# A mixer's parts over thirteen groups at a time, and another order inside a group, in an attention phase on one core

## What is computed

```python
# graph attention (8 heads of 32)
score = einsum('ehd,ehd->eh', q[edge_dst], k[edge_src])
score = clip(score / sqrt(32), -10, 10)
ex    = exp(score - smax[edge_dst])
den   = segment_sum(ex, edge_dst)
wv    = segment_sum(ex / den[edge_dst] * v[edge_src], edge_dst)
# ball mixer, from the same normalized rows, one sequence position
h   = relu(batchnorm(conv(logmap0(proj(x)))))
cat = concat([t, pointwise(depthwise(t))])        # t from h
vk  = einsum('ngdl,ngel->ngde', v, relu(k))
out = einsum('ngde,ngdl->ngdl', vk, relu(q)) / (sum(v) + 1e-15)
fx  = proj(expmap0(logmap0(proj(expmap0(out))) @ w_res + b_res))
```

## Time and profile before

| | us |
|---|---|
| median of 3 runs | 3400.9 (3397.17 to 3411.24) |
| the profiled execution | 3413.5 |
| its span in the trace | 3411.8 |
| mean granted TensorE clock | 0.859 |
| busy: PE / PE weight loads | 2540.0 (74%) / 2051.8 (60%) |
| busy: DVE / ACT / POOL | 2133.1 (63%) / 1269.2 (37%) / 1238.6 (36%) |

### The profile page before, as it was taken

How to read it: one execution, slowest core, us unless ns; L and a number is a source line. 1 busy time by engine, 2 the same in 40 slices (tenths; PEclk the granted TensorE clock), 3 DMA queues, 4 the chain that set the end, 5 groups by cost and what they waited for, 6 DMA issues and landing times. The chain is left out here.

```text
span 3411.8 us, 62980 instructions
## 1 busy us (share of the span) xinstructions
PE 2540.0 (74%) x17412; PEld 2051.8 (60%) x17412; DVE 2133.1 (63%) x4254; ACT 1269.2 (37%) x2593; POOL 1238.6 (36%) x971
## 2 busy tenths in 40 slices
PE   6546555777579999766767686767655976999997
PEld 5424344666457777543656564656544865899986
DVE  7655455644468888754686867777775566444455
ACT  1432211311245455423535353444433343444441
POOL 0058786688400000002646464655623001211125
PEclk9968855888779999777979898888977986999998
DMA  5238574233100000044647465555634004466633
GB/s 142 84 85 222 143 206 122 67 82 83 42 19 19 10 18 18 25 148 126 159 112 170 121 163 131 152 149 141 160 94 117 0 0 162 147 237 226 236 121 87
DMA packets 251663, 387.61 MB, mean 114 GB/s; under 512 B 117456, under 2 KB 175661, under 8 KB 246878
## 3 DMA queue, kind: packets, MB, share of 16 engines
q0 software_dynamic: 151392, 170.67, 20.5%
q1 hardware_dynamic: 87224, 202.62, 18.9%
q10 hardware_dynamic: 12864, 12.06, 1.2%
HBM read 323.76 MB, written 60.56 MB: 113 GB/s over the span
## 5 line engine op out<-in xcount | busy, mean ns | idle before, releaser
L921 POOL DMA_INDIRECT ms_got<-gather,edge_src x400 | 531.1, 1328 | 164.7 <-issue 120.2
L2120 POOL DMA_INDIRECT xz_rows<-gather_kv,edge_src x205 | 257.5, 1256 | 220.5 <-PE ab_total L2292 165.2
L2120 POOL DMA_INDIRECT ab_gkv<-gather_kv,edge_src x200 | 266.5, 1333 | 187.6 <-PE ab_total L2292 132.9
L969 PE MATMUL ms_total<-ms_got,ms_hot 125*125 125x256 f16 x1040 | 177.3, 335 | 177.4 <-DVE ms_hot L942 126.8
L969 PEld LDWEIGHTS ms_total<-ms_got,ms_hot 125*125 x1040 | 150.3, 171 | 212.2 <-issue 211.8
L1635 ACT ACTIVATE ex_h<-ex_up,ex_now 128x313 f32<-128x313 f32 (+1 forms) x320 | 196.1, 613 | 196.7 <-PE ex_up L700 189.3
L3027 DVE CAST moe_hidden<-moe_h 128x256 f16<-128x256 f32 (+1 forms) x336 | 101.5, 302 | 203.6 <-ACT moe_h L2964 201.0
L2266 PE MATMUL ab_picked<-y_rows,ab_zeros 125*125 125x512 f16 (+1 forms) x246 | 73.8, 417 | 204.6 <-DVE ab_qk L2365 184.4
L1851 POOL MEMSET br_one<- 125x1 f16 x1 | 0.1, 106 | 604.4 <-POOLq L125 604.4
L2964 ACT ACTIVATE moe_h<-moe_up,wring 128x256 f32<-128x256 f32 (+1 forms) x336 | 163.1, 487 | 128.6 <-PE moe_up L700 85.7
L2275 PE MATMUL ab_picked<-y_rows,xz_rows 125*125 x1060 | 178.0, 329 | 35.6 <-issue 18.0
(11 more groups left out here) (527 smaller groups left out, 6090.3 us busy)
## 6 DMA issues: line engine op xcount, KB each, us to landing
wring<-wsplit SPq DMA_DIRECT2D x33, 2052.0 KB
ab_dsts<-in_dst SPq DMA_DIRECT2D x83, 305.2 KB
wsplit<-mix_split SPq DMA_DIRECT2D x32, 512.0 KB
mix_raw<-in_L_ffn_W1p SPq DMA_DIRECT2D x16, 512.0 KB
mix_raw<-in_L_ffn_W2p SPq DMA_DIRECT2D x16, 512.0 KB
results<-moe_made SPq DMA_DIRECT2D x32, 256.0 KB, 7.6
ms_got<-gather,edge_src POOLq DMA_INDIRECT x400
gather_kv<-qkv_out SPq DMA_DIRECT2D x5, 1120.0 KB
```

The source lines that it names most:

```text
L921: pool.indirect_dma_start(out=self.got[:, s, j, :], out_offset=None, in_=self.m.gather0, in_offset=bass.IndirectOffsetOnAxis(ap=self.m.edg ...
L969: ins = pe.matmul(self.total[:, visit % 2, 0:C], self.hot[:, visit % RING, j, :], self.got[:, s, j, p * C:(p + 1) * C], start=(j + p == 0) ...
L2120: pool.indirect_dma_start(out=gkv[s][:, j, 0:2 * C], out_offset=None, in_=m.gather_kv, in_offset=bass.IndirectOffsetOnAxis(ap=m.edge_src[: ...
```

## The change

Nothing is computed in another way. Two things are laid out anew.

First, the stages. PERIOD is 13 and a chunk now has 27 stages, so that two chunks (three at one group of each period) are in work at once: `chunks_at(n)` lists them, older first. JOIN, WEIGH, OUT and LAST take every second group. The seven DVE operations of a weighing are divided over three groups: four at the stage, the reciprocal one group later, the last two products two groups later; `ksum` has two buffers for that. At multiples of 13 a stage 0, a reciprocal (stage 13) and a tail (stage 26) come together.

Second, the order within a group. DVE weighs and makes the one-hots of n before it multiplies for n + 1; PE makes the totals of n before the picks of n + 2. ACT keeps its order.

```diff
-    PERIOD = G // CHUNKS
-    CONV, JOIN, WEIGH, OUT, LAST, TAIL = 0, 3, 8, 9, 10, 15
+    PERIOD = 13
+    CONV = range(0, 3)
+    JOIN, WEIGH, OUT, LAST = (range(at, at + 2 * J, 2) for at in (3, 12, 15, 17))
+    ROOTS, TAIL = 25, 26
+
+    def chunks_at(n):
+        return [(c, n - c * PERIOD) for c in range(CHUNKS) if 0 <= n - c * PERIOD <= TAIL]
...
-        ksum = ph.sb("ksum", [R, GN])
+        ksum = ph.sb("ksum", [R, 2, GN])
...
-                    if g % PERIOD == CONV + 8 and g // PERIOD < CHUNKS - 1:
-                        sp.wait_ge(s_up, g // PERIOD * UNITS + len(PARTS) * OB)
-                        rows(g // PERIOD + 1)
-                    if g % PERIOD == 6 and 0 < g // PERIOD < CHUNKS:
-                        mixed(g // PERIOD - 1)
+                    for c in range(CHUNKS - 1):
+                        if g == c * PERIOD + 8:
+                            sp.wait_ge(s_up, c * UNITS + len(PARTS) * OB)
+                            rows(c + 1)
+                        if g == c * PERIOD + TAIL + 4:
+                            mixed(c)
...
                 for n in range(G):
-                    part(n // PERIOD, n % PERIOD)
+                    for c, s in chunks_at(n):
+                        part(c, s)
                     bounds = group_bounds(act, m, n + 3)
                     weights(n + 1, (n + 1) % GATHERED)
                     one_hots(n + 3, (n + 3) // 2, (n + 3) % 2, bounds)
...
                 for n in range(G):
-                    c, s = divmod(n, PERIOD)
                     ahead = group_bounds(pe, m, n + 2)
                     bounds = group_bounds(pe, m, n)
-                    part(c, s, False)
+                    for c, s in chunks_at(n):
+                        part(c, s, False)
+                    sums(n, n % GATHERED, bounds)
                     pick_q(n + 2, ahead)
-                    part(c, s, True)
-                    sums(n, n % GATHERED, bounds)
+                    for c, s in chunks_at(n):
+                        part(c, s, True)
...
                 def late(c, s):
-                    if s == WEIGH:
+                    for j, at in enumerate(WEIGH):
+                        q, w = cat[:, j, 0, :, :], cat[:, j, 2, :, :]
+                        if s == at + 1:
+                            b.link(dve.reciprocal(w, w))
+                        if s == at + 2:
+                            b.link(dve.tensor_tensor(q, q, w, ALU.mult))
+                            b.link(dve.tensor_tensor(q, q, repeat_last(ksum[:, j % 2, :], HD), ALU.mult))
+                            b.done(s_o)
+                    if s == WEIGH[0]:
...
-                        b.link(dve.reciprocal(w, w))
-                        b.link(dve.tensor_tensor(q, q, w, ALU.mult))
-                        b.link(dve.tensor_tensor(q, q, repeat_last(ksum[:, :], HD), ALU.mult))
-                        b.done(s_o)
...
                 for n in range(G):
-                    c, s = divmod(n, PERIOD)
-                    early(c, s)
-                    multiply(n + 1)
+                    for c, s in chunks_at(n):
+                        early(c, s)
                     weigh(n)
                     bounds = group_bounds(dve, m, n)
-                    visits(n, s, bounds)
+                    visits(n, n, bounds)
+                    multiply(n + 1)
                     scores(n + 1)
-                    late(c, s)
+                    for c, s in chunks_at(n):
+                        late(c, s)
```

More of the change, by code:

```diff
@@ L11 @@
+import itertools
 from contextlib import ExitStack, contextmanager
@@ L2182, in weights, with squared @@
                         .then_inc(s_exp, 1)
-                def squared(source, into, before):
-                    act.wait_ge(s_square, before + AHEAD)
+                squares = itertools.count(AHEAD)
+                def squared(source, into):
+                    done = next(squares)
+                    act.wait_ge(s_square, done)
                     act.activation(junk[:, 0:source.shape[-1]], source, ACT.Square, accum_out=into)\
                         .then_inc(s_square, 1)
-                SQUARES = 4 * J + J + J
+                    return done + 1
                 def convolved(c, u):
@@ L2201, in joined @@
                     bank = unit[0:R, u % 2, 0:HALF]
-                    squared(bank, s2[:, k, j:j + 1], c * SQUARES + (j * 4 + k))
+                    squared(bank, s2[:, k, j:j + 1])
                     parts = bank.rearrange("p (g q d) -> p q g d", q=3, d=HD)
@@ L2207, in part @@
                 def part(c, s):
-                    if CONV <= s < CONV + 3:
-                        for u in range(4 * (s - CONV), 4 * (s - CONV) + 4):
+                    if s in CONV:
+                        for u in range(4 * s, 4 * s + 4):
                             convolved(c, u)
-                    if JOIN <= s < JOIN + J:
+                    if s in JOIN:
                         for k in range(4):
-                            joined(c, s - JOIN, k)
-                    if s == WEIGH:
+                            joined(c, JOIN.index(s), k)
+                    if s == WEIGH[0]:
                         act.wait_ge(s_sum, c + 1)
                         act.activation(nr[:, 0:2, :], s2[:, 1:4:2, :], ACT.Sqrt).then_inc(s_norm, 1)
-                    if LAST <= s < LAST + J:
-                        j = s - LAST
+                    if s in LAST:
+                        j = LAST.index(s)
                         t = c * J + j
@@ L2224, in part @@
                         act.activation(fx[:, j, :], o_bank[0:R, 0:C], ACT.Copy).then_inc(s_raw, 1)
-                    if OUT <= s < OUT + J:
-                        j = s - OUT
+                    if s in OUT:
+                        j = OUT.index(s)
                         t = c * J + j
@@ L2230, in part @@
                                        ACT.Copy).then_inc(s_oc, 1)
[L2231 to L2234, removed]
+                        turned[c] = squared(cat[:, j, 0, :, :].rearrange("p g d -> p (g d)"), s2[:, 4, j:j + 1])
+                    if s == ROOTS:
+                        act.wait_ge(s_square, turned[c])
                         act.activation(nr[:, 2, :], s2[:, 4, :], ACT.Sqrt).then_inc(s_norm2, 1)
@@ L2238, in part @@
                             act.wait_ge(s_fx, c * J + (j + 1))
-                            squared(fx[:, j, :], s2[:, 5, j:j + 1], c * SQUARES + (5 * J + j))
-                        act.wait_ge(s_square, c * SQUARES + (6 * J + AHEAD))
+                            done = squared(fx[:, j, :], s2[:, 5, j:j + 1])
+                        act.wait_ge(s_square, done)
                         a_.link(act.activation(nr[:, 3, :], s2[:, 5, :], ACT.Sqrt))
                         act.activation(nr[:, 4, :], nr[:, 3, :], ACT.Tanh).then_inc(s_tanh, 1)
+                turned = {}
                 act.wait_ge(s_node, 3)
@@ L2315, in part @@
                 def part(c, s, late):
-                    if CONV <= s < CONV + 3:
-                        if s == CONV and not late:
+                    if s in CONV:
+                        if s == 0 and not late:
                             pe.wait_ge(s_rows, (c + 1) * 16)
                             pe.sem_inc(s_pace, 1)
-                        for u in range(4 * (s - CONV) + 2 * late, 4 * (s - CONV) + 2 * late + 2):
+                        for u in range(4 * s + 2 * late, 4 * s + 2 * late + 2):
                             convolve(c, u)
-                    if JOIN <= s < JOIN + J:
+                    if s in JOIN:
                         for k in range(2 * late, 2 * late + 2):
-                            join(c, s - JOIN, k)
-                    if LAST <= s < LAST + J and not late:
-                        t = c * J + (s - LAST)
+                            join(c, JOIN.index(s), k)
+                    if s in LAST and not late:
+                        t = c * J + LAST.index(s)
                         pe.wait_ge(s_oc, t + 1)
@@ L2331, in part @@
                         ins.then_inc(s_f, 1)
-                    if OUT <= s < OUT + J and late:
-                        j = s - OUT
+                    if s in OUT and late:
+                        j = OUT.index(s)
                         t = c * J + j
@@ L2425, in late @@
                         b.link(dve.tensor_tensor(nr[:, 6, :], nr[:, 6, :], nr[:, 5, :], ALU.mult))
-                    if WEIGH <= s < WEIGH + J:
-                        j = s - WEIGH
-                        gamma = nr[:, 6, j:j + 1]
+                    if s in WEIGH:
+                        j = WEIGH.index(s)
+                        gamma, total_k = nr[:, 6, j:j + 1], ksum[:, j % 2, :]
                         q, k, w = (cat[:, j, i, :, :] for i in range(3))
-                        b.mark(dve.tensor_reduce(ksum[:, :], k, AX_X, ALU.add))
+                        b.mark(dve.tensor_reduce(total_k, k, AX_X, ALU.add))
```

(6 more changed lines are left out.)

## The result

The changed kernel takes 3540.89 us (median of 4 runs, 3535.43 to 3549.66) against 3402.16 us for the kernel before in the same comparison: a ratio of 1.041, 95% interval 1.038 to 1.044. It is slower by 139 us, where 47 were forecast and the range ended at 3515. The direction was right, the size was a third of what came.

What follows compares the result with a forecast made beforehand. The prediction took a new ring through PE, ACT and DVE to bound the attention phase. Execution 3413.5 us, plus 24 for rings and 23 for the clock, gave 3460, or 3448 us against the runs' median; range 3375 to 3515.

Steps and rivals of the forecast that it cites:

- The new ring through PE and ACT: One-hots, totals, picks, late units, exp, weighing: join and convolution groups 10.75 us, OUT 9.73, longer than DVE's 9.3 to 9.6.
- the sum said + 24: All groups and second visits of the phase, 940 us against 913.5, less 3 at the end, with PE at full clock.
- I take + 23, a little below the middle of 0 and 88, since PE will be busy between the two: Clock's cost on 350 us of PE work in the rings: 0 at join-window clock 1.00, 88 at weighing-window clock 0.80.
- this case runs from 3395 to 3515: Bounds of the first case, chance 0.52, forecast 3448 us, from the clock's ends and 0.5 us per ring either way.
- the 29 us of the rings: Uncertainty of the ring lengths: 0.5 us either way for each of 58 rings.
- Second visits: PE goes to a second visit's first total at once: 24 times 3.94 us against some 6.0, saving about 50 us.
- The exp's wait, 50 to 90 us: Sign of being right: DVE's weighing newly waits for ACT's exp, 1 to 1.5 us in join, convolution and OUT groups.
- DMA and POOL cost nothing: Gathers get a group more to land, so DVE's 72 us of waits for them should go.
- Before, the product (n+2) went ahead on DVE while the exp came; now nothing of the next group can: On DVE, the reason given for the ring: weighing (n+1) waits for the exp with no product ahead; no separate size.
- The rival that DVE's own ring decides: Weighing on DVE, groups 12 to 75: the exp is there when DVE's late part ends; 3280 us, chance 0.20.
- The rival that the clock stays at 0.80 or second visits wait as before (0.14): PE's clock stays low, or PE is in mixer units when first one-hots come: 3500 to 3530 us, chance 0.14.
- The rival of a shorter ring: Picks overlap the totals' end, ring 0.4 us shorter, clock near 1.00: 3400 us, no change, chance 0.14.

Runs made afterwards that it cites:

- ACT's order: The changed kernel with one call moved on ACT, the next group's exp ahead of the mixer's part instead of behind it: 3403.44 us, ratio 0.999 to the kernel before.
- PE's late units: The changed kernel with PE's late mixer units moved ahead of the totals, ACT untouched: 3344.62 us, ratio 0.982 to the kernel before.
- stages alone: The changed kernel with the order inside a group put back on DVE and PE, stages spread as in the change: 3342.22 us, ratio 0.980 to the kernel before.
- ten zeros: The changed kernel with ten never-read products of zeros on PE ahead of every group's totals: 3443.93 us, ratio 1.010 to the kernel before.
- two variants of it: The changed kernel with the old order on DVE and PE (3342.22 us), and, second, with PE's late mixer units ahead of the totals (3344.62 us).

## Why the prediction was right, and where it was wrong

- **The new ring through PE and ACT**: right, and shown by three openings at different places (ACT's order 137 us, PE's late units 196 us, stages alone without it). At full clock (0.99 to 1.00 over these groups) its sum holds: OUT 9.73 forecast, 9.64 measured; join with one visit and one pick visit 10.75 forecast, 10.62 to 10.67 in four groups of the changed kernel and the same with ten zeros. A tail is 13.9 in the forecast and 13.5 to 14.1 measured, at a clock of 0.78 to 0.82. The run with ten zeros stands at + 35 where the sum said + 24; whether the other 11 are the zeros in the way is not shown. So the direction was no luck.
- **"I take + 23, a little below the middle of 0 and 88, since PE will be busy between the two"**: this step failed, the clock's term of the sum. Taking PE's idle time away with ten zeros gives 97 us back, and the change's 139 less that run's 35 is 104: the term measures some 100 us. Two things were wrong in it. First, PE is not busy between the two windows (22.0 and 18.6 us of 25) but less than in either, 17.1, since it waits 312 us for one-hots, and the clock of the phase is 0.81. The prediction's own working with 0.81 gives an estimate of + 82. Second, I spread a window's mean over 350 us of PE work, but the low clock does not fall evenly: the new order makes PE idle 3.2 us on average (311.8 us, 98 times) just ahead of the totals, which stand in the ring, and there it falls (72 of 104 at 0.50 to 0.73, 32 at 1.00). The totals alone grew by 128.5 us, while the picks gained 41 (178.0 to 136.6 us). So 88 was no upper bound for the clock.
- **"this case runs from 3395 to 3515"**: the upper end is added wrong. It has the clock's 88 but not the 29 us of the rings: 3413.5 - 12.6 + 24 + 88 + 29 = 3542, which the measured 3541 just reaches. That doesn't mend the + 23.
- **Second visits, "Against some 6.0 before this saves about 50 us"**: wrong by the same cause. The forecast was a wait of about 60 us; it was 98.6 with the slow totals, and 61.6 in the run with ten zeros.
- **The exp's wait, 50 to 90 us**: 187.8. With the zeros it is 88.8, and 42 more are idle time without a releaser.
- **DMA and POOL cost nothing**: right; gathers are waited for 17 us instead of 72.
- **"Before, the product (n+2) went ahead on DVE while the exp came; now nothing of the next group can"**: the weight was wrong. With only PE turned and the product ahead on DVE the time is 3610 us. The totals' place on PE closes the ring, not the product's.
- **The rival that DVE's own ring decides**: false of this kernel, and what two variants of it reached (groups of 8.9 to 9.7 us). Its time was too low (3280; measured 3342 and 3345), with 95 us for second visits already in it. A part is that an empty group takes 6.4 us in the second of them, where it had 5.9; the rest is open. Interleaving the two regimes by the stages alone gains 2.0%.
- **The rival that the clock stays at 0.80 or second visits wait as before (0.14)**: it came nearest. Both of its conditions came about (0.81; 98.6 us of waiting against 109.2), but each was priced by itself, at 3500 to 3530, and not the two together. **The rival of a shorter ring**: false, the ring is 0.1 us shorter than the sum and not 0.4.

## What to carry to other kernels

Follow a loop's dependencies once around over all engines, with the place of each step in its engine's queue: an engine that is nearly full in some windows is not what decides if a ring through it and two others is longer. When an edit puts a wait directly ahead of matmuls on that ring, price those matmuls at the trace's lowest clock too (here 0.50), not at a window's mean alone: here 72 of 104 took over 2.9 us, where those at 1.00 took 2.39 to 2.49. And try the parts of a change apart: here the stages gave 2% and the order took 6%.

## What was not expected of the hardware

Adding 800 useless products (187 us of PE's time) ahead of a wait made the program 97 us faster, because the totals after it went from 3.8 to 2.7 us on average (392.0 and 277.9 us over 104 visits). The clock changes inside a group and back again: in the rows above the total at 2041.47 runs at a clock of 1.00 (2.48 us), that at 2051.11 at 0.50 (4.76), and the picks from 2056.73 at 0.93 (20 products in 2.53 us, as 10 in 1.26 before), with 1.00 from 2057.50 on. The windows of 25 us shown have 0.66 to 0.89, means over stretches at 1.00 and at 0.50: of the 2180 windows of 0.5 us in the phase 1302 have 1.00, 747 have 0.50 and the other 131 lie between.
